# Two buffers for the backward maxima of a segment softmax, and backward steps moved by a slot on three engines

## The reference

```
x = x + segment_sum((h * W)[src], dst)                      # layer 0
x = x + two SAGE layers (means over neighbours, 64 -> 128 -> 64)
x = x + relu(segment_sum(alpha * (h_fc[src] + eh), dst) + h_fc @ loop_W)
    # eh = edge_attr @ W_fcr.T;  alpha = softmax of eh over the edges of one target
x = x + mean over neighbours of (h @ W.T + b)
```

## Time and profile before

| | |
|---|---|
| median of three runs | 7272.27 us (7261.26 to 7274.29) |
| span of the profiled execution (its page gives no other time for it) | 7292.8 us |
| start of the first and of the last backward scan | 1381.2 and 3098.1 us |
| busy share of the span | PE 73%, PEld 67%, DVE 64%, ACT 51%, POOL 45% |
| granted clock of TensorE, mean | 0.887 |

### The profile page before, as it was taken

The page is one execution under the profiler, slowest core; times in us unless marked ns, Lnnn a source line. Parts: engine busy times, 40 slices in busy tenths (PEclk is TensorE's granted clock), DMA queues, the critical chain, the costliest instruction groups (busy, mean ns, idle before and its releaser), DMA issues.

```text
span 7292.8 us, 127838 instructions
## 1 busy us (share of the span) xinstructions
PE 5329.4 (73%) x47490; PEld 4851.8 (67%) x47491; DVE 4674.7 (64%) x6110; ACT 3735.6 (51%) x2908; POOL 3306.2 (45%) x3416
## 2 busy tenths in 40 slices
PE   0110577776776777789999999975688788887887
PEld 0110455565555556689999999975577677777776
DVE  9785466656565665678888788863455555555554
ACT  0111234455555555568887788740254455554565
POOL 0006777777777770010000100027777777777740
PEclk9555899888888888899999999987899999999998
DMA  9974799877777777666666666643577677766685
GB/s 342 373 256 51 219 310 312 251 218 208 214 218 208 215 214 215 206 190 198 194 196 182 190 196 196 197 135 81 121 158 153 143 157 153 158 153 143 150 145 105
DMA packets 1647798, 1407.88 MB, mean 193 GB/s; under 512 B 902034, under 2 KB 1511827, under 8 KB 1646751
## 3 DMA queue, kind: packets, MB, share of 16 engines
q1 hardware_dynamic: 840469, 987.40, 45.9%
q10 hardware_dynamic: 694608, 354.86, 19.3%
q0 software_dynamic: 112128, 57.61, 5.0%
HBM read 878.67 MB, written 363.28 MB: 170 GB/s over the span
## 4 chain that ended last, share of the span: by engine, by line
PE 47%; DVE 19%; ACT 10%; issue 9%; DMA 7%; POOL 6%; DVEq 2%; ACTq 1%; SPq 0%; POOLq 0%
PE pair L1609 25%; PE pair L1720 8%; PE wide L1744 6%; POOL cells L1056 3%; DMA pm_d<-u 3%; ACT u L1495 3%; PE wide L1570 3%; DVE u L433 3%; DVE u L434 3%; POOL u L1089 2%; DVE u L705 2%; PE flip L1592 2%; ACT u L1363 2%; ACT wide L1345 2%; ACT batch L1495 1%
## 5 line engine op out<-in xcount | busy, mean ns | idle before, releaser
L1335 ACT ACTIVATE u<-u 128x1792 bf16<-128x1792 uint8 x1286 | 2139.4, 1690 | 1291.9 <-PE pair L1609 711.2
L1609 PE MATMUL pair<-tab,u 128*128 128x192 bf16 (+1 forms) x28812 | 2595.9, 252 | 22.8 <-ACT u L1335 22.8
L1609 PEld LDWEIGHTS pair<-tab,u 128*128 128x128 bf16 x28812 | 2518.3, 100 | 102.6 <-ACT u L1335 24.4
L608 DVE TENSOR_REDUCE u<-u 128x1792 bf16<-128x1792 uint8 x870 | 1735.8, 2016 | 877.8 <-PE pair L1609 774.5
L1089 POOL DMA_INDIRECT u<-zrows,stage x1664 | 1605.8, 965 | 1326.6 <-DMA zrows<-batch 783.1
L1056 POOL DMA_INDIRECT cells<-val,idx x1664 | 1614.4, 970 | 1087.0 <-issue 1063.2
L1720 PE MATMUL pair<-u 128*128 x4880 | 940.1, 350 | 404.7 <-DVE u L862 387.7
L1720 PEld LDWEIGHTS pair<-u 128*128 128x128 f32 x4880 | 856.8, 204 | 480.3 <-issue 478.9
L1570 PE MATMUL wide<-u,wbd 128*128 128x512 f32 (+1 forms) x1120 | 488.7, 565 | 408.9 <-DVE u L705 294.7
L1495 ACT ACTIVATE u<-u 128x1792 bf16<-128x1792 uint8 x317 | 525.0, 1684 | 317.1 <-PE wide L1744 312.6
L1570 PEld LDWEIGHTS wide<-u,wbd 128*128 128x128 f32 x1120 | 213.7, 212 | 597.8 <-issue 585.4
(11 more groups left out here) (255 smaller groups left out, 4800.6 us busy)
## 6 DMA issues: line engine op xcount, KB each, us to landing
u<-cells SPq DMA_DIRECT2D x2058, 224.0 KB, 3.2
cells<-zt SPq DMA_DIRECT2D x98, 1568.0 KB, 15.7
u<-in_ea SPq DMA_DIRECT2D x280, 384.0 KB
ex_d<-u ACTq DMA_DIRECT2D x280, 384.0 KB
u<-ex_d SPq DMA_DIRECT2D x208, 512.0 KB
pm_d<-u ACTq DMA_DIRECT2D x140, 384.0 KB
u<-pm_d SPq DMA_DIRECT2D x140, 384.0 KB, 3.8
u<-gate_d ACTq DMA_DIRECT2D x280, 96.0 KB
```

The costliest lines, as they stand in the source:

```text
L608: return V.tensor_reduce(to, of.unsqueeze(3), AX.X, ALU.max)
L1335: return S.activation(to, of, ACT.Copy)
L1609: mm = M(acc(t // 2 * 2 + b)[:, 0:width], ring[:, q % nr, (b * CK + k) * P:(b * CK + k + 1) * P], table[:, j, 0:width], start=j == 0 and b ...
```

## The change

The difference of one step and the scan of the next no longer share a buffer: `mx` becomes a list of two, the second in an unused part of `batch`, and the scan waits for the difference of two steps before. On each of three engines some backward steps change their slot. DVE swaps the last scan and the last product of a tile. PE takes features(st) into slot 0, and the second turns of a tile behind chunk 0 of the next. ACT takes maxima(st+1) into slot 0, maxima(st+2) into slot 4 behind the conversion, copies(st) into slot 5 ahead of exponential(st+1), and the copies of the tile's second step into slot 1 of the next tile, behind exponential(st). SP's queue, the conversions and the chunks keep their slots. The order after it:

```diff
-        mx, xe = area[6], area[7]
+        mx, xe = [area[6], batch[:, 6 * B7 * F:6 * B7 * F + SB]], area[7]
...
                 if st:
                     dve.wait_ge(b_carry, st)
-                    dve.wait_ge(b_sub, st)
+                if st >= 2:
+                    dve.wait_ge(b_sub, st - 1)
                 dve.wait_ge(b_max, st + 1)
-                V.tensor_tensor_scan(mx[:, ::-1], b_gate[h][:, ::-1], eh[h][:, ::-1], carry[:, :], ALU.add, ALU.max).then_inc(b_scan, 1)
+                V.tensor_tensor_scan(mx[h][:, ::-1], b_gate[h][:, ::-1], eh[h][:, ::-1], carry[:, :], ALU.add, ALU.max).then_inc(b_scan, 1)
...
                     elif c == 4:
                         bwd_sub(st + 1)
-                    elif c == 5:
+                    elif c == 5 and st + 2 < STEPS:
+                        bwd_scan(st + 2)
+                    elif c == 6:
                         bwd_mul(st + 1)
-                    elif c == 6 and st + 2 < STEPS:
-                        bwd_scan(st + 2)
...
+                    if c == 0:
+                        maxima(st + 1)
                     if c == 1:
                         exps(st)
-                        maxima(st + 1)
-                    if c == 4:
+                        if st:
+                            turned_out(st - 1)
+                    if c == 4 and st + 2 < STEPS:
+                        maxima(st + 2)
+                    if c == 5:
                         turned_out(st)
-                    if c == 5:
                         exps(st + 1)
-                    if c == 5 and st + 2 < STEPS:
-                        maxima(st + 2)
-                    if c == 6:
-                        turned_out(st + 1)
+            turned_out(STEPS - 1)
             root()
...
-                    elif c == 1:
+                    elif c == 0:
                         bwd_features(st)
+                    elif c == 1 and st:
+                        bwd_turns(st - 1)
                     elif c == 3:
                         bwd_features(st + 1)
                     elif c == 4:
                         if st == 0:
                             pe.wait_ge(s_prep, marks["sums", 0])
                         bwd_turns(st)
-                    elif c == 6:
-                        bwd_turns(st + 1)
                     chunk(0, t, c, WC, tab[0])
+            bwd_turns(STEPS - 1)
```

More of the change, by code:

```diff
@@ L702, in bwd_scan @@
                     dve.wait_ge(b_carry, st)
-                    dve.wait_ge(b_sub, st)
+                if st >= 2:
+                    dve.wait_ge(b_sub, st - 1)
                 dve.wait_ge(b_max, st + 1)
-                V.tensor_tensor_scan(mx[:, ::-1], b_gate[h][:, ::-1], eh[h][:, ::-1], carry[:, :], ALU.add, ALU.max).then_inc(b_scan, 1)
+                V.tensor_tensor_scan(mx[h][:, ::-1], b_gate[h][:, ::-1], eh[h][:, ::-1], carry[:, :], ALU.add, ALU.max).then_inc(b_scan, 1)
                 dve.wait_ge(b_scan, st + 1)
-                V.tensor_copy(carry[:, :], mx[:, 0:1]).then_inc(b_carry, 1)
+                V.tensor_copy(carry[:, :], mx[h][:, 0:1]).then_inc(b_carry, 1)
             def bwd_sub(st):
                 dve.wait_ge(b_mm, st + 1)
-                V.tensor_tensor(b_pm[st % 3], eh[st % 2], mx, ALU.subtract).then_inc(b_sub, 1)
+                V.tensor_tensor(b_pm[st % 3], eh[st % 2], mx[st % 2], ALU.subtract).then_inc(b_sub, 1)
             def bwd_mul(st):
```

## The result

The changed kernel takes 7499.28 us (median of four runs, 7498.53 to 7511.09); the kernel before, with one more run by then, 7273.28 us. The ratio is 1.0309 with a 95% interval of 1.0292 to 1.0326: slower by 226 us. The forecast was 7445, in a range of 7300 to 7560.

A forecast was written before the change was run, and what follows sets the result against it. The prediction took a ring of waits between PE, ACT and DVE as the bound: 35 x 2.3 + 35 x 2.6 = 171 us, plus 2 at the sweep's end, clock loss unchanged, gave +173, 7445 us, range 7300 to 7560.

The forecast's parts named there:

- The ring: Backward tile's loop of waits between PE, ACT and DVE: odd tile 21.3 to 23.6 us, even 21.55 to 24.2.
- 171 + 2: Forecast loss in us: 35 odd tiles at 2.3 plus 35 even at 2.6, and about 2 at the sweep's end.
- The forecast wait for the copies: PE's wait in the turns' third group for ACT's copies: about twice as long, near 2 us, in both turns.
- 26.7 to 27.7: Sign of being right: mean us a tile between backward scans, from 23.9 + 1.15 + 2.12 = 27.2.
- The buffers and the swap: Two maxima buffers save and cost nothing; DVE's scan ahead of the product takes second product and second turns off the ring.
- The covers: Moved product and maxima run behind other engines' work without cost; maxima's load lands by 23.75 us of the ring at worst.
- The clock: Loss a backward tile from PE's lower granted clock: taken as unchanged, bounded from 2.12 less to 5.2 us more.
- The two pull against each other: PE's shorter part of the ring against its four idle spells a tile instead of three; clock loss kept at 2.12.
- The 2.12: Us a tile left in the kernel before, 24.70 - 1.15 - 21.43, put down to the lower clock.
- 1.15: Us a tile for the tails: ten of 70 tiles have 8.0 us more on DVE.
- The clock falls after every turn: Rival: slow PE chunks behind both turns and after the scan's wait, 4.8 us a tile lost, 7630 us; chance 0.13.
- Faster: Rival: ACT's first copies start 0.91 us behind the turns, the tile takes 20.1 us, 7180 us in all; chance 0.06.

The follow-up runs named there:

- filled kernels: Matmuls of zero weights put on PE ahead of its waits: on the changed kernel 7312.62 us, on the kernel before 7158.33 us.
- split kernel: Changed kernel with the third group of turns split off on PE and put behind the next chunk: 7045.38 us.

## Why the prediction was right, and where it was off

*The ring: right.* That ACT's copies behind a conversion and other work hold the third group, and with it chunks 1 and 4, DVE's conversions and both scans, is shown from two sides: moving the copies ahead takes back 210 us, and letting the chunks pass the wait takes back 454. The filled kernels show the ring nearly without the lower clock: tiles without a tail come out within 0.1 us of it in the old order, and 0.1 and 0.2 under it in the new one. The two orders then differ by 7312.6 - 7158.3 = 154 us, for the 171 + 2 of the sum. The forecast wait for the copies, near 2 us, is the median of 1.96. The mean tile of 27.69 us lies at the upper edge of the 26.7 to 27.7 that were called right; what pushed it there is mostly the clock, as worked out below.

*The buffers and the swap: right.* Nothing for the buffers; the swap +127 in the old order, -32 in the new.

*The covers: right.* The scans didn't wait for maxima, and the end of the sweep, from the last scan to the next pass's first chunk load, takes 18.6 us instead of 16.9, for the +2 of the forecast.

*The clock: mechanism right, size off.* The step was "The two pull against each other; I take the loss of before, 2.12". Filling gives back 187 us in the changed kernel, 2.7 a tile, and 111 us in the one before, 1.6 a tile. So the loss did not stay equal: by these runs it grew by 1.1 us a tile, 76 us. Taken from the scans of the profiled executions it grew by 0.8: the filled sweeps need 25.09 and 22.94 us a tile (1374.6 to 3118.2 and 1370.3 to 2964.7), the others 27.69 and 24.70. The 154 of the ring and these 76 add up to 230 by the way they are worked out, so that they meet the measured 226 is no further proof. The 2.12 itself was a remainder, and not all of it was the clock: with the clock filled, the old order still takes 22.94 - 21.43 = 1.5 us a tile over the ring where the prediction had 1.15 for the tails.

Why the loss grew is argued, not shown: PE stands idle in four spells a tile instead of three, and that seems to pull harder than the shorter PE part of the ring. One reading behind this term was wrong. The prediction says that the 2.82 us now come before slow features; in the earlier trace rows the features behind the wait of 2.82 are fast (1.53), and the slow ones (2.90) stand behind the wait of 2.96. That the sum came out 53 us under the measured 226 is this term and the ring's 154 for 173, of opposite sign: the total is closer than its parts.

*The rivals.* "The clock falls after every turn" at 7630 was too much, but the result lies on its side of the forecast. The rule of the Trainium skill ("TensorE: Matmul & The Clock Gate", PE-mode transpose), that transposes don't count as busy for the clock as matmuls do, is not decided here: filling put matmuls into the idle time next to the transposes and into the wait for the scan at once, and no run separates idle time from transposes. "Faster" failed as stated: in the half tile shown the first copy starts 2.60 us behind the turns, not 0.91. But once the chunks pass the wait, the new order is the better one.

## What to carry to other kernels

In an ordered queue ask not only what an instruction waits for, but what stands behind it: moving a group of transposes one chunk further back was worth 454 us, clock included, while PE's waits ahead of it stayed as long in all. A schedule in which no engine is full can be added up start to start along the ring of waits. Check the sum against one undisturbed tile of the kernel before; here it then gave the tiles of the new order to within 1%, once the clock was kept up. An idle spell of PE can cost twice, once as a wait and once as slow work behind it: here filling the spells gave back 187 and 111 us. That second price needs a term of its own for the new order, and can't be taken over from the old one.

## What was not expected of the hardware

Matmuls that compute nothing, put into PE's waits, made both kernels faster: 187 us and 111 us, with the granted clock of the sweep going from 0.85 and 0.87 to 0.97. In the changed kernel PE was busy 167 us longer by the profile and the sweep was 194 us shorter. In the split kernel, where PE's waits no longer set the pace, the same trick gained nothing (7057.36 against 7045.38).
